# Cross-attention layer: feed-forward interleaved by half slots with the last attention, x's low halves on GpSimd, W2's halves made beside the attention

## The reference, cut to what matters

```python
# x, ctx: (16, 512, 512) float32; 16 heads of 32; feed-forward width 2048
q = (x @ Wq + bq); k = (ctx @ Wk + bk); v = (ctx @ Wv + bv)      # split into heads
scores = einsum('bhqd,bhkd->bhqk', q, k) / sqrt(32)
scores = where(j < i, scores, -1e30)                            # strictly below the diagonal
attn = softmax(scores); attn[:, :, 0, :] = 0
ctx_out = einsum('bhqk,bhkd->bhqd', attn, v)
x1  = layer_norm(x + ctx_out @ Wo + bo, ln1_g, ln1_b)
out = layer_norm(x1 + relu(x1 @ W1 + b1) @ W2 + b2, ln2_g, ln2_b)
```

## Time and profile before

| | us |
|---|---|
| median of 3 runs | 2662.8 (2660.74 to 2662.99) |
| the profiled execution, its time | 2661.86 |
| its span, first to last instruction | 2660.0 |
| PE busy in it | 2596.9 (98%) |
| DVE busy | 2077.8 (78%) |
| POOL busy | 1556.8 (59%) |
| ACT busy | 1525.6 (57%) |
| mean granted TensorE clock | 0.987 of full |

### The profile page before, as it was taken

One profiled execution on the slowest core, in us unless ns is written; L12 is line 12 of the kernel. 1 busy time (PEld: TensorE's weight loads), 2 busy tenths in 40 slices (PEclk: granted clock), 3 DMA queues, 4 the chain that ended last, 5 costly groups with the idle time before them and its releaser, 6 DMA issues.

```text
span 2660.0 us, 62128 instructions
## 1 busy us (share of the span) xinstructions
PE 2596.9 (98%) x22540; PEld 2237.7 (84%) x22540; DVE 2077.8 (78%) x5171; ACT 1525.6 (57%) x2945; POOL 1556.8 (59%) x1721
## 2 busy tenths in 40 slices
PE   7999999999999999878999999999999999999998
PEld 5888888888888888757888888888888888888887
DVE  6889888988888888788767767676767676767675
ACT  4777787787777877677343434343434344444433
POOL 3777777766666666566555545454555544454543
PEclk9999999999999999978999999999999999999999
DMA  7666655565555655556132222222222222222220
GB/s 194 156 154 157 162 152 155 153 151 149 146 141 147 152 140 141 138 135 176 42 70 50 69 52 67 54 64 57 57 64 57 64 57 64 56 65 56 64 57 25
DMA packets 439556, 273.35 MB, mean 103 GB/s; under 512 B 299648, under 2 KB 334400, under 8 KB 439248
## 3 DMA queue, kind: packets, MB, share of 16 engines
q1 hardware_dynamic: 438288, 267.79, 40.4%
q10 hardware_dynamic: 960, 1.57, 0.3%
HBM read 109.86 MB, written 57.67 MB: 63 GB/s over the span
## 4 chain that ended last, share of the span: by engine, by line
PE 92%; DVE 3%; SPq 1%; issue 1%; DMA 1%; POOL 1%; ACT 1%; ACTq 0%; DVEq 0%; POOLq 0%
PE h_ps L1369 25%; PE acc L1385 22%; PE lin_ps L708 13%; PE front L1355 6%; PE lin_ps L704 6%; PE max_ps L683 6%; PE st_ps L730 6%; PE o_ps L750 4%; PE o_ps L752 3%; PE st_ps L765 2%; POOL prob_lo L429 1%; DVE W L1276 1%; SPq L847 0%; ACTq L492 0%; SPq L354 0%
## 5 line engine op out<-in xcount | busy, mean ns | idle before, releaser
L429 POOL TENSOR_TENSOR prob_lo<-probs,prob_hi 128x512 f16<-128x512 f32 (+1 forms) x768 | 784.4, 1035 | 371.7 <-ACT prob_hi L508 366.9
L1369 PE MATMUL h_ps<-x_halves,W 128*128 128x256 f16 x6144 | 756.4, 273 | 2.0 <-ACT hf L1183 2.0
L1385 PE MATMUL acc<-W,hs 128*128 128x256 f16 x5376 | 669.6, 273 | 1.0 <-DVE hs L1329 1.0
L1369 PEld LDWEIGHTS h_ps<-x_halves,W 128*128 128x128 f16 x6144 | 596.5, 98 | 87.8 <-issue 16.8
L1183 ACT ACTIVATE hf<-h_ps,b1s,scale_evac 128x256 f32<-128x256 f32 x512 | 284.8, 562 | 583.5 <-PE h_ps L1369 581.6
L664 DVE CUSTOM_DVE_ANT_0 max_ps<-max_ps,mask_q 128x128 f32<-128x128 f32 (+3 forms) x1024 | 485.5, 505 | 129.3 <-PE max_ps L683 113.2
L1385 PEld LDWEIGHTS acc<-W,hs 128*128 128x128 f16 x5376 | 525.9, 98 | 62.2 <-issue 1.5
L506 ACT ACTIVATE probs<-st_ps 128x512 f32<-128x512 f32 (+1 forms) x768 | 406.5, 529 | 244.2 <-PE st_ps L765 227.2
L1109 POOL TENSOR_TENSOR hf<-hf 128x256 f32<-128x256 f32 x256 | 237.7, 928 | 500.6 <-ACT hf L1183 500.4
L508 ACT ACTIVATE prob_hi<-st_ps 128x512 f16<-128x512 f32 (+1 forms) x768 | 406.8, 530 | 0.0
L1329 DVE TENSOR_TENSOR hs<-hf,hs 128x896 f16<-128x896 f32 x256 | 279.1, 1109 | 142.9 <-ACT hs L1172 142.9
(11 more groups left out here) (119 smaller groups left out, 3761.9 us busy)
## 6 DMA issues: line engine op xcount, KB each, us to landing
heads<-stage SPq DMA_DIRECT2D x756, 128.0 KB, 2.5
raw<-in_xT SPq DMA_DIRECT2D x64, 256.0 KB, 3.1
o_in<-ctx_rows SPq DMA_DIRECT2D x256, 64.0 KB, 2.5
x_in<-in_x SPq DMA_DIRECT2D x32, 512.0 KB, 4.0
x_rows<-x SPq DMA_DIRECT2D x64, 256.0 KB, 2.1
o_in<-x_rows SPq DMA_DIRECT2D x256, 64.0 KB, 2.4
out<-y SPq DMA_DIRECT2D x32, 512.0 KB, 3.1
raw<-in_cT SPq DMA_DIRECT2D x60, 256.0 KB, 3.9
```

Source lines behind the costliest of these rows:

```text
L429: pool.tensor_tensor(prob_lo[:, k % 4, 0:w], probs[:, k % PROBS, 0:w], prob_hi[:, k % 4, 0:w], ALU.subtract).then_inc(pl_done, 1)
L1369: last = pe.matmul(h_ps[:, f % 2, 0:T], W1[:, aw, j, f * P:(f + 1) * P], x1_halves[:, item.parity, aa, j, :], start=(j == 0 and m == 0), s ...
L1385: last = pe.matmul(acc_products[:, n, :], hs[:, p % HS, aa, n, :], W2[:, p, aw, n, :], start=(p == 0 and m == 0 and n % 2 == 0), stop=(p = ...
```

## The change

Six edits come together.

1. `side_by_side` loses its pace: after each attention slot from slot 38 on it advances the feed generator once, and every feed generator now yields twice in a slot. The rate stays one feed slot in two attention slots, in halves.
2. Norm 1 on DVE is four pieces: sums and variance with the residual, `centre`, `inverse_root`, `shift` (one slot later, step `NORM1 + 1`).
3. The low half of x in attention moves from DVE to POOL (four 128x512 instructions an item, three slots apart), with a semaphore `x_lo` of its own.
4. The scan moves earlier: `SCAN_LOAD` 39 (was 42), `SCAN_LOOK` 46 (was 50), `MIX` from 43 (was 46).
5. W2's halves are made beside the attention, in items 0 to 7: DVE derives a scale of the pair for each partition in four small instructions behind the scan; ACT makes the high half in two instructions (slots 51 and 58), DVE the low half in two (53 and 59), in `raw`; SP stores them as float16 (four DMAs in place of three).
6. `feed` then splits only 16 chunks (W1), four in three slots; W2 comes by eight DMAs of 128x3584 float32 words that ACT issues. The power of two of each pair is given back through the scale and bias of `h_ps`'s evacuation.

The number and shapes of the matmuls stay as they are.

```diff
-        if at > start and (at - start) % pace == 0:
+        if at > start:
             next(second)
...
-    SCAN_LOAD = 42
-    SCAN_LOOK = SLOTS + 2
-    MIX = SLOTS - 2
-    MIX_STORE = SLOTS + 11
+    SCAN_LOAD = 39
+    SCAN_LOOK = SLOTS - 2
+    MIX = SLOTS - 5
+    HALF_HI = (SLOTS + 3, SLOTS + 10)
+    HALF_LO = (SLOTS + 5, SLOTS + 11)
+    HALF_STORE = (SLOTS + 6, SLOTS + 12)
...
+                for j in range(KT):
+                    for item in x_splits(window, s, j, 1 + j, 0):
+                        wait_for(pool, hi_done, NCHUNK, item, chunk_of("x", j) + 1)
+                        pool.tensor_tensor(acts["x"][:, 1, j, :], raw[:, j, :], acts["x"][:, 0, j, :], ALU.subtract
+                                           ).then_inc(x_lo, 1)
...
+                        act.activation(hi, src, ACT.Copy, scale=bounds.row_value[:, 1:2]).then_inc(bounds.half_hi, 1)
...
+                    if item.n < bounds.pairs:
+                        value, scale = bounds.row_value[:, 0:1], bounds.row_value[:, 1:2]
+                        power = bounds.row_power[:, item.n:item.n + 1]
+                        dve.tensor_scalar(value, bounds.part[:, :], 1e-12, None, ALU.max).then_inc(bounds.row_step, 1)
+                        dve.wait_ge(bounds.row_step, 4 * item.n + 1)
+                        dve.tensor_scalar(power.bitcast(U32), value.bitcast(U32), 0x7F800000, None, ALU.bitwise_and
+                                          ).then_inc(bounds.row_step, 1)
+                        dve.wait_ge(bounds.row_step, 4 * item.n + 2)
+                        dve.reciprocal(value, power).then_inc(bounds.row_step, 1)
+                        dve.wait_ge(bounds.row_step, 4 * item.n + 3)
+                        wait_for(dve, bounds.half_hi, 2, item, 0)
+                        dve.tensor_scalar(scale, value, SUM_TOP, None, ALU.mult).then_inc(bounds.row_step, 1)
+                for g in range(2):
+                    for item, _ in due(window, s, SLOTS, B, HALF_LO[g]):
...
+                        wait_for(dve, bounds.half_hi, 2, item, g + 1)
...
+                        dve.scalar_tensor_tensor(out=lo, in0=src, scalar=bounds.row_value[:, 1:2], in1=hi,
+                                                 op0=ALU.mult, op1=ALU.subtract).then_inc(bounds.half_lo, 1)
...
-                    for item in x_splits(window, s, j, 2):
-                        split(item, "x", j)
...
-    def split_slot(n):
-
-        return n if n < KT else PROJ + (n - KT) * 2 // 3
+    W2_LOAD = (10, 11, 13, 15, 20, 21, 23, 25)
+
+    def split_half(n):
+
+        return 2 * n if n < KT else 2 * PROJ + (n - KT) * 3 // 2
...
+                for p in range(PAIRS):
+                    if (window, s) == (W2_LOAD[p] // SLOTS, W2_LOAD[p] % SLOTS):
+                        act.wait_ge(*(before.heads_read + [before.o_read])[heads_group(p)])
+                        act.wait_ge(bounds.halves_stored, 64 * PAIRS)
...
+                        act.dma_start(W2[:, p, :, :, :], bounds.w2_halves[:, p, :, :, :]).then_inc(w2_loaded[p], 16)
...
+                split_weights(window, s, 0)
+                residual(window, s, 1)
+                for item, _ in due(window, s, SLOTS, CHUNKS, NORM1 + 1):
+                    shift(0, item, [x1[:, item.parity, u, :] for u in range(U)])
+                yield
+                split_weights(window, s, 1)
+                residual(window, s, 0)
+                for item, _ in due(window, s, SLOTS, CHUNKS, RES + U - 1):
+                    centre(0, item, [x1[:, item.parity, u, :] for u in range(U)])
                 for item, _ in due(window, s, SLOTS, CHUNKS, NORM1):
-                    normalise(0, item, [x1[:, item.parity, u, :] for u in range(U)])
+                    inverse_root(0, item)
```

More of the change, by code:

```diff
@@ L78, in wait_for, with side_by_side @@
         eng.wait_ge(sem, per * item.n + c)
-def side_by_side(first, second, start, pace):
+def side_by_side(first, second, start):
     at = 0
@@ L266, in attention, with x_splits @@
     o_out = sem("o_out")
-    def x_splits(window, slot, j, behind=0):
+    def x_splits(window, slot, j, behind=0, first_behind=0):
         rest = after_first(due(window, slot, SLOTS, B, X_SPLIT + 2 * j + behind))
-        first = due(window, slot, SLOTS, 1, FIRST_X_SPLIT + 2 * j + behind)
+        first = due(window, slot, SLOTS, 1, FIRST_X_SPLIT + 2 * j + first_behind)
         return [item for item, _ in (*rest, *first)]
@@ L500, in scalar @@
                         split(item, "x", j)
+                for g in range(2):
+                    for item, _ in due(window, s, SLOTS, B, HALF_HI[g]):
+                        if item.n >= bounds.pairs:
+                            continue
+                        _, parts = bounds.mixes(raw)
+                        src, hi, _ = parts[g]
+                        if g == 0:
+                            wait_for(act, bounds.row_step, 4, item, 4)
+                            wait_for(act, bounds.halves_stored, 64, item, 0)
+                        else:
+                            wait_for(act, bounds.half_lo, 2, item, 1)
+                        wait_for(act, bounds.mixed, 5, item, (3, 5)[g])
+                        act.activation(hi, src, ACT.Copy, scale=bounds.row_value[:, 1:2]).then_inc(bounds.half_hi, 1)
                 for item, k in due(window, s, SLOTS, B, ST_AT, SLOTS):
@@ L950, in feed @@
     w_lo = sem("w_lo")
-    b1_scaled = sem("b1_scaled")
+    w2_loaded = [sem(f"w2_loaded{p}") for p in range(PAIRS)]
+    h_scales = sem("h_scales")
     bv_hi = sem("bv_hi")
@@ L1018, in part_of, with weights_due @@
     def part_of(n, part):
-        if n >= KT and order[n - KT][0] == "w2":
-            return chunks[n][1][part]
         return chunks[n][1][:, part, :]
-    def raw_of(n):
-        if n >= KT and order[n - KT][0] == "w2":
-            return raw_slot(n).rearrange("p (h n) -> p h n", h=2)
-        return raw_slot(n)
-    def weights_due(window, slot, behind=0):
+    def weights_due(window, slot, half):
         if window <= BACK:
-            return [n for n in range(len(chunks)) if split_slot(n) + behind == slot + SLOTS * window]
+            return [n for n in range(len(chunks)) if split_half(n) == 2 * (slot + SLOTS * window) + half]
         return []
@@ L1036, in feed @@
     scale_w1, scale_w2, scale_x1, scale_h = (bounds.scale[:, n:n + 1] for n in range(4))
-    h_evac, y_evac, y_less = bounds.evac[:, 0:1], bounds.evac[:, 3:4], bounds.less[:, 0:1]
-    weight_scale = [None] * KT + [{"w1": scale_w1, "w2": scale_w2}[w] for w, _ in order]
+    y_evac, y_less = bounds.evac[:, 3:4], bounds.less[:, 0:1]
     acc_products = acc[:, :, :].rearrange("p b (h n) -> p (b h) n", h=2)
@@ L1115, in scalar, with split_weights @@
     def scalar(act):
+        def split_weights(window, s, half):
+            for n in weights_due(window, s, half):
+                act.wait_ge(raw_loaded[n % RAW], 16 * (n // RAW + 1))
+                if n == 0:
+                    act.wait_ge(*before.inputs_read)
+                if n == KT:
+                    act.wait_ge(bounds.ready, 2)
+                if n < KT:
+                    act.activation(part_of(n, 0), raw_slot(n), ACT.Copy).then_inc(w_hi, 1)
+                else:
+                    act.activation(part_of(n, 0), raw_slot(n), ACT.Copy, scale=scale_w1).then_inc(w_hi, 1)
         def root(norm, item):
@@ L1218, in normalise, with shift @@
                                      ).then_inc(ln_root[norm], 1)
+        def shift(norm, item, tiles):
+            z = rs[:, norm, 2, :]
             wait_for(dve, ln_root[norm], 1, item, 1)
@@ L1321, in vector @@
                         statistics(1, item, u, y[:, u, :])
-                    variance(1, item, [y[:, u, :] for u in range(U)])
+                    variance(1, item)
+                    centre(1, item, [y[:, u, :] for u in range(U)])
                 for item, _ in due(window, s, SLOTS, CHUNKS, NORM2):
-                    normalise(1, item, [y[:, u, :] for u in range(U)])
+                    inverse_root(1, item)
+                    shift(1, item, [y[:, u, :] for u in range(U)])
                 for item, k in due(window, s, SLOTS, CHUNKS, FFN1 + 4, FT):
```

201 lines of the change are left out of this document (112 added, 89 removed).

## The result

The changed kernel takes 2708.97 us (median of 4 runs, 2705.13 to 2710.2), the kernel before 2662.89 beside it: ratio 1.0169, interval 1.0154 to 1.0184, 46 us. The forecast was 2667 and the range ended at 2684.

The account below looks back on a forecast made before the run. PE (98% busy) was taken as the bound: 2661.86 us minus 16.5 gained in the transition plus 20.3 paid in the attention gave 2665.7, as run median 2667; own range 2657 to 2676, wider range 2643 to 2684.

Parts of the forecast that it names:

- (d): Attention, x's low halves on POOL: late prob_lo costs 0.35 us in eight items, 0.8 in seven; 2.8 + 5.6 us paid.
- (e): Attention, scan in slot 46 with four small instructions behind it: PE pays 1.1 us in seven items, 7.7 us.
- (f): Attention, W2's halves on ACT and DVE: PE pays 0.6 us in seven items, 4.2 us, first half nothing.
- (a): Transition, DVE's scales block four slots earlier, in slot 8 without maxima, and earlier SP moves: gain 3 us.
- (b): Transition, 1122 to 1213 us: six fewer chunks split and norm 1 in parts shorten the stretch, gain 9 us.
- (c): Transition, 1213 to 1262 us: the other 22 chunks go, PE's 5.8 us idle shrinks, gain 4.5 us.
- the pauses add up: Rival: attention delays follow one another, seven windows paying 4 us, eight 0.8; transition gives 14; 2683 us; chance 0.16.

Follow-up runs that it names:

- e10: Changed kernel with the shift of norm 1 half a slot later, behind the attention's onorm: 2710.67 us.
- e7: Changed kernel with feed again interleaved a whole slot to two and norm 1 in one piece, W2's halves kept beside the attention: 2708.42 us.
- e2: Kernel before the change with only x's low halves moved to GpSimd (POOL): 2677.68 us.
- e3: Changed kernel with x's low halves back on DVE, two slots behind their high halves: 2698.23 us.
- e4: Changed kernel with the four small instructions behind the scan run for the first pair of W2 only: 2701.56 us.
- e5: Changed kernel with scan and row operations back in slot 2, scales in slot 12, W2's first high half one slot later: 2690.46 us.
- e12: Changed kernel with the scan in slot 2 and W2's low halves written by a one-input instruction (wrong values): 2681.84 us.
- e11: Changed kernel with scan in slot 2 (loaded in 42), x's low halves in slots 34, 39, 42, 44, Strassen sums in 46, 47, 1, 4, 7: 2705.42 us.
- e14: Changed kernel with scan in slot 2 (SCAN_LOAD 41), x's low halves in 34, 39, 42, 44, Strassen sums in 45, 47, 1, 4, 7: 2707.24 us.

## Why the prediction was wrong, step by step

The direction of each cost was right, their sizes were not, and the gain mostly failed: about 4 us in place of 16.5. The sum of the costs was 20.3 us; by slots and in all fifteen items it is 40.6, of which (d) 17.5, (e) 13.2 and (f) 9.9, and by the periods 45. Steps as the prediction names them:

**(a) The scales, 3 us: about 1 by the first stretch (8.2 us lost against 9.4).** In slot 8 there is no unit of maxima, but `osum` and `onorm` of a head are there, and PE waits 3.75 us for `onorm` at 1139.9 where it had waited 3.0 for a maximum. Three of the small instructions took 0.63 to 1.11 us; the second of the two shown has a single input.

```profile
1134.01 1.11 DVE L571 SCALAR_TENSOR_TENSOR scale_value<-scan_top,scale_evac 128x1 f32<-128x1 f32 x1
1135.35 0.90 DVE L576 TENSOR_SCALAR scale_power<-scale_value 128x4 uint32<-128x4 uint32 x1
```

**(b) The middle of the transition, 9 us: nothing (43 us lost, 42.2 before).** This is the largest single failure of the gains. I read the wait of 4.73 us in the earlier trace rows as one for `osum`, with the shift ahead of it, and took its going for a gain. PE does not wait for `osum` but for `onorm` one slot later, and the new order puts the shift between the two:

```profile
1232.24 0.56 DVE L646 TENSOR_REDUCE osum<-o_ps 128x128 f32<-128x384 f32 x1
...
1233.35 1.37 DVE L1311 SCALAR_TENSOR_TENSOR x<-x,rs,vec_be 128x512 f32<-128x512 f32 x2
1234.64 0.28 DVE L657 TENSOR_TENSOR onorm<-osum,o_ps 128x128 f32<-128x128 f32 x1
```

The wait became 5.25 us. e10 shows the mechanism (3.9 us with the shift behind `onorm`), and that the `heads<-rows` wait was next in line. The six chunks fewer relieved an engine that was not the last link: DVE's load fell only from 71.9 to 70.6 of 91 us. Gain by the order seems to be there only together with the missing chunks (e7, 6.4 us between single executions), and norm 1 in parts costs 1 to 4 us in pure feed (1383.3 to 1386.8 against 1382.4 to 1382.7), a stretch that I had counted at nothing as part of a tail that is "hardly touched".

**(c) 4.5 us: right**, 3.9 by the idle time.

**(d) x's low halves, 0.35 us an item, 0.8 with W2's sums behind them: 0.81 and 1.57.** The place and the room of 0.57 us were right, a duration was wrong. The sum put the short `prob_lo` ahead of x at its plain 0.67 us and came out 0.2 to 0.3 us late; it lasts 1.20 there, and 0.25 + 0.53 is the 0.8 that PE pays. The sum had moved that instruction to a new time without asking what DVE runs then. The 0.76 at slot 46, which only the first seven items have, is the fourth low half with a Strassen sum directly behind it: it is absent in e2, where the sum stands three slots later, and nearly so in e3 (0.15), where x is on DVE. I had seen this pair, but let the delay of slot 40 shelter it; the two add up.

**(e) The scan block, 1.1 us in seven items: 1.03 at slot 47 in these, and 0.74 in the other eight, which I had at nothing.** Without the row operations 0.31 of the first remain (e4); with the scan in slot 2 it is 0.47 and nothing (e5). What I did not see is that the block falls behind DVE's row step of slot 44, and that the low half of x moved to slot 43 would hold an instruction there that was already in the program. I priced locks for the instructions that the change adds, not for those that they land beside. This is the step that failed in the attention, in (d) and in (e): the costs did not shelter one another, they joined.

**(f) The halves, 0.6 us: 1.4 in slots 8, 10 and 13.** The form with one input takes away all that e5 still has of it at slots 10 and 13, 0.92 (e12). I had looked at DVE's slack only. What PE paid was POOL: a `prob_lo` held for 0.7 us by the 1.28 us of the second low half, and a Strassen sum of 1.50 us in place of 0.74 beside the first half, which I had counted at nothing.

By the Trainium skill, "SBUF — State Buffer", sections "Summary: rules for kernel authors" and "Who interferes with whom", the second of two instructions that contend for the port pair that VectorE and GpSimd share is blocked until the first has finished. The row step agrees (1.21 us at 755.30); the scan's small maximum in e11 and e14 does not, since its 3.00 to 3.03 us span three more of POOL's instructions. By the second of these sections a VectorE instruction with at most one input in SBUF does not contend with GpSimd outside its modes that use two ports. Six of seven items of e12 agree; the seventh, and L663 of e3 with its 0.64 us, show that one input alone is no guarantee. The prediction gave the rule 15.6 us in place of 11.9 for (e) and (f); by slots the two came to some 23.

The rival "the pauses add up" named the mechanism (the first seven periods 4 us each, measured 4.5; the others 0.8, measured 1.5), and I gave it 0.16 because the places that I had looked at seemed to have room. With its own numbers it would have said 2697 but for the 14 us that it let the transition give.

Left open: what in norm 1's parts makes single `hs` late in pure feed; whether and why the order gains in the transition only without W2's chunks; what decides when a held instruction has to wait for more than the first; and what one shorter high half on ACT would save, which was not tried.

## What to carry to other kernels

Before moving work to an engine that shares something with another, list the other engine's instructions beside the new slot, the old ones too, and what stands right behind each: a 0.18 us instruction that becomes 1.22 costs 0.75 us an item with the scan close behind it, and nothing without (e5). Give each instruction of the receiving engine's queue the duration that it has beside its neighbour, not its plain one: 0.67 against 1.20 us for one `prob_lo` was the difference between 0.25 and 0.8 us an item. To take a step out of a wait, find the last link of the chain that the wait names (`onorm`, not `osum`), and check that the step really leaves it.

## What the runs showed of the hardware that I had not expected

A VectorE instruction with two inputs in SBUF that is held beside GpSimd mostly ends with the first GpSimd instruction (0.18 us became 1.21), but can be held for far longer: 0.16 us became 3.00 to 3.03 in all seven items of e11 and of e14, until GpSimd had a gap. In all fourteen it began 0.04 to 0.08 us before the end of a GpSimd instruction (244.92 against 244.98 in the row shown); whether that decides is not shown.

The wait goes the other way too: GpSimd's `prob_lo` took 1.87 us beside a VectorE instruction of 1.28 with two inputs, and its plain 1.16 and 0.67 beside one of 1.27 with a single input (e12). That one took 0.75 us in one of the seven items, and then the short `prob_lo` took 1.24 in place of 0.67.
